# Four graph layers on one core: in the last layer VectorE masks messages by edge type, and sources are turned one chunk ahead

## The reference

```python
src = x[edge_src]
parts = [relu(x)]
for t in range(3):
    msg = relu(src @ W_e[t].T + b_e[t])
    msg = where((edge_type == t)[:, None], msg, 0)
    parts.append(segment_sum(msg, edge_dst))
agg = concatenate(parts, axis=1)
for t in range(3):
    o = agg @ W_n[t].T + b_n[t]
    updated = where((node_type == t)[:, None], o, updated)
x = layernorm(x + updated + x)
```

## Time and profile before

| | us |
|---|---|
| median of three runs | 2155.61 |
| the profiled execution | 2157.94 |
| its span | 2155.8 |
| busy in the span: TensorE, VectorE, ScalarE, GpSimd | 1613.2, 1479.8, 1087.1, 1385.2 |
| last layer: first product of its messages to the end of the span | 1714.1 to 2155.8 |

### The profile page before, as it was taken

How to read it: one execution, slowest core, us unless ns; L and a number is a source line. 1 busy time by engine, 2 the same in 40 slices (tenths; PEclk the granted TensorE clock), 3 DMA queues, 4 the chain that set the end, 5 groups by cost and what they waited for, 6 DMA issues and landing times.

```text
span 2155.8 us, 23908 instructions
## 1 busy us (share of the span) xinstructions
PE 1613.2 (75%) x6303; PEld 993.3 (46%) x6303; DVE 1479.8 (69%) x4219; ACT 1087.1 (50%) x2688; POOL 1385.2 (64%) x1060
## 2 busy tenths in 40 slices
PE   3777777777776377776776677777778499999995
PEld 1444444444444255555554344444444145555553
DVE  4788999988889377677776667776677444444453
ACT  0466666666666466777667243444343323233322
POOL 6888877788884667776660656555664146656663
PEclk7688888888888687888778788888889699999998
DMA  4333333333331344444443333333232122222221
GB/s 122 83 84 91 92 90 92 94 91 90 95 91 53 94 120 142 148 141 141 140 139 98 100 93 89 99 99 95 86 94 73 53 58 72 63 60 64 71 60 27
DMA packets 150726, 198.86 MB, mean 92 GB/s; under 512 B 54874, under 2 KB 82844, under 8 KB 150592
## 3 DMA queue, kind: packets, MB, share of 16 engines
q1 hardware_dynamic: 92992, 173.20, 25.7%
q0 software_dynamic: 57600, 24.15, 6.6%
HBM read 140.85 MB, written 70.88 MB: 98 GB/s over the span
## 4 chain that ended last, share of the span: by engine, by line
PE 58%; ACT 17%; issue 12%; DVE 7%; POOL 3%; DMA 2%; SPq 1%; POOLq 0%; ACTq 0%; DVEq 0%
PE po L1148 19%; PE pb L1342 10%; PE pt L1133 7%; ACT x L918 6%; PE po L1143 4%; ACT res L918 3%; PE pc L1133 3%; ACT st L973 3%; PE po L1207 2%; PE pb L1154 2%; DVE masked L838 2%; ACT do L918 1%; PE pc L1238 1%; ACT so L918 1%; PE pb L1379 1%
## 5 line engine op out<-in xcount | busy, mean ns | idle before, releaser
L434 POOL DMA_INDIRECT xs<-target_rows,slot_all x300 | 405.7, 1352 | 246.7 <-DMA xs<-source_rows 97.1
L918 ACT ACTIVATE x<-y,nmr,rst 125x128 f32<-125x128 f32 x800 | 318.5, 481 | 80.1 <-DVE nmr L671 80.0
L1148 PE MATMUL po<-wnt,rt 128*125 128x384 f32 x800 | 310.9, 537 | 0.2 <-ACT rt L948 0.2
L1133 PE MATMUL pt<-ident,x 125*128 125x125 f32 x800 | 144.2, 310 | 199.0 <-issue 182.4
L449 POOL TENSOR_TENSOR y<-xin,bias_bc 125x512 f32<-125x512 f32 x100 | 133.7, 1338 | 205.9 <-DMA xin<-in_x 201.4
L1148 PEld LDWEIGHTS po<-wnt,rt 128*125 128x125 f32 x800 | 174.2, 218 | 117.8 <-issue 40.8
L1342 PE MATMUL pb<-masked,wr 128*128 128x500 f32 x400 | 218.1, 709 | 1.5 <-DVE masked L838 1.5
L441 POOL DMA_INDIRECT out_rows<-do,last_all x100 | 120.2, 1202 | 145.2 <-ACT do L918 107.9
L838 DVE SCALAR_TENSOR_TENSOR masked<-rel,st 128x500 f32<-128x500 int32 x200 | 121.6, 670 | 132.8 <-ACT st L973 132.8
L1133 PEld LDWEIGHTS pt<-ident,x 125*128 125x128 f32 x800 | 105.2, 162 | 232.5 <-issue 207.0
L1143 PE MATMUL po<-ball,ones_bf 128*125 128x512 bf16 (+1 forms) x512 | 163.4, 452 | 51.1 <-DVE sel L688 48.7
(11 more groups left out here) (182 smaller groups left out, 3211.0 us busy)
## 6 DMA issues: line engine op xcount, KB each, us to landing
xin<-in_x SPq DMA_DIRECT2D x100, 250.0 KB
out_rows<-res SPq DMA_DIRECT2D x100, 250.0 KB
source_rows<-so SPq DMA_DIRECT2D x75, 250.0 KB
target_rows<-do SPq DMA_DIRECT2D x75, 250.0 KB
xs<-source_rows SPq DMA_DIRECT2D x75, 250.0 KB
xd<-target_rows SPq DMA_DIRECT2D x75, 250.0 KB
same<-same_d SPq DMA_DIRECT2D x75, 250.0 KB
aux<-start_d SPq DMA_DIRECT2D x25, 250.0 KB
```

What stands on the lines that cost most here:

```text
L434: return nc.gpsimd.indirect_dma_start(out=to, out_offset=None, in_=table, in_offset=bass.IndirectOffsetOnAxis(ap=index, axis=0), bounds_ch ...
L918: last = A(to[:, j, :], y[:, j, :], ACT.Identity, scale=rst[s][:, k:k + 1], bias=nmr[s][:, k:k + 1])
L1133: last = nc.tensor.transpose(tile_of(to, j), rows_[:, j, :], ident[0:R, 0:R])
L1148: last = mm(po[0:R, j * 512:j * 512 + NT * D], left(j), wnt[:, k, :, :].rearrange("k t d -> k (t d)"), start=False, stop=stop, skip_group_ ...
```

## The change

The offsets go: neither their table, its stores, its loads, nor the one-row products are there any more. The edge types are loaded for each chunk into all 128 partitions (`rel`, 250 KB) behind `same`, on the same semaphore, and VectorE multiplies each message by "type equals t" in place, all three types ahead of the three scans. TensorE turns the sources of chunk `c + 2` between the second and the third of the sums of chunk `c`, and ScalarE copies them at the end of its loop turn, ahead of `results3`. `sources3` no longer waits for the messages' products.

```diff
-            for t in range(NT):
-                sp.dma_start(off_d[t].rearrange("(p t) -> p t", t=PM), off_p[:, t, :]).then_inc(s_scr, 16)
-            sp.wait_ge(s_scr, 16 * (2 + NT))
+            sp.wait_ge(s_scr, 32)
...
             def sources3(c):
                 sp.wait_ge(q["tS"], at(c - 1))
-                sp.wait_ge(q["pM"], at((c - 1) * NT))
                 sp.dma_start(flat(xs[b]), rows(s_rows[2])[c]).then_inc(q["ld"][b], 16)
-                sp.dma_start(off[b][:, :, :], off_d[:, cols(c)][None]).then_inc(q["ld"][b], 16)
             def targets3(c):
                 sp.wait_ge(q["rd"], at(c - 1))
+                sp.wait_ge(q["vM"], at((c - 1) * NT))
                 sp.dma_start(flat(xd[b]), rows(d_rows[2])[c]).then_inc(q["aux"][b], 16)
                 sp.dma_start(same[b][:, :], to_all(same_d, c)).then_inc(q["aux"][b], 16)
+                sp.dma_start(rel[b][:, :], to_all(etype3, c)).then_inc(q["aux"][b], 16)
...
             def message_sums(c):
-                dve.wait_ge(q["aux"][b], counted(c, 32))
+                dve.wait_ge(q["aux"][b], counted(c, 48))
                 dve.wait_ge(q["pR"], at(c - 1))
                 for t in range(NT):
                     dve.wait_ge(q["eX"], c * NT + (t + 1))
+                    V.scalar_tensor_tensor(out=masked[:, t, :], in0=rel[b][:, :], scalar=float(t), in1=masked[:, t, :],
+                                           op0=ALU.is_equal, op1=ALU.mult).then_inc(q["vM"], 1)
+                for t in range(NT):
+                    dve.wait_ge(q["vM"], c * NT + (t + 1))
                     scan(m, t, same[b][:, :], masked[:, t, :], ALU.mult, ALU.add,
...
             for c in range(EC + 1):
                 if there(c + 1):
                     messages3(c + 1)
...
                 if there(c + 1):
                     targets3(c + 1)
+                if there(c + 2):
+                    evacuate_sources(c + 2, 3, 0)
                 if c >= 1:
                     results3(c - 1)
...
+            def turn_sources3(c):
+                pe.wait_ge(q["g"][b], counted(c, 16 * T))
+                pe.wait_ge(q["eD"], c)
+                turn(pt, xs[b]).then_inc(q["tS"], 1)
             def messages(c):
                 pe.wait_ge(q["eS"], c + 1)
                 for t in range(NT):
                     pe.wait_ge(q["eX"], at((c - 1) * NT + t + 1))
-                    mm(bank[5 + t][:, 0:C], ones_bf[0:1, :], off[b][0:1, t, :], start=True, stop=False)
-                    mm(bank[5 + t][:, 0:C], wet[:, t, :], st[:, :], start=False, stop=True).then_inc(q["pM"], 1)
+                    mm(bank[5 + t][:, 0:C], wet[:, t, :], st[:, :], start=True, stop=True).then_inc(q["pM"], 1)
             def targets(c):
-                pe.wait_ge(q["aux"][b], counted(c, 32))
+                pe.wait_ge(q["aux"][b], counted(c, 48))
                 pe.wait_ge(q["eS"], c + 1)
                 turn(pt, xd[b]).then_inc(q["tD"], 1)
...
                 for k in range(NT):
+                    if k == NT - 1 and there(c + 2):
+                        turn_sources3(c + 2)
                     pe.wait_ge(q["vA"], c * NT + (k + 1))
                     last = types(lambda j: run_tile(sums, k, j), 1 + k, stop=k == NT - 1)
```

More of the change, by code:

```diff
@@ L68, in gnn_kernel @@
     rdeg_d = nc.dram_tensor("rdeg_d", [1, E], F32).ap()
-    off_d = nc.dram_tensor("off_d", [NT, E], BF16).ap()
     slot_d = nc.dram_tensor("slot_d", [N, 1], I32).ap()
@@ L106, in gnn_kernel @@
         src_all, dst_all, nxt_all, last_all = (sb(n, [R, EC, T], I32) for n in ("src_all", "dst_all", "nxt_all", "last_all"))
-        ty = sb("ty", [R, PM], I32)
         same_p, start_p = (sb(n, [R, PM]) for n in ("same_p", "start_p"))
@@ L111, in gnn_kernel @@
         before_p, carry = sb("before_p", [R, 1]), sb("carry", [1, R + 1])
-        off_p = sb("off_p", [R, NT, PM], BF16)
         fill = sb("fill", [R, N // R], I32)
@@ L135, in gnn_kernel @@
         rel = two(sb, "rel", [D, C], I32)
-        off = two(sb, "off", [1, NT, C], BF16)
         run, run2 = sb("run", [D, 3, C + 1]), sb("run2", [D, 3, C + 1])
@@ L165, in gnn_kernel @@
         SINGLE = ("tS tD eS eD eL pA pB pR vA vE vL eX nS nD nF yb eN", "tS tD eS eD pR vA nS nD rd",
-                  "tS eS pM pR vA vM nD", "tS tD eS eD pM pR vA eX vN nD rd")
+                  "tS eS pM pR vA vM nD", "tS tD eS eD pM pR vM vA eX vN nD rd")
         PAIRS = ("aux g stS stD sc", "ld aux g stS stD", "ld aux rl g gi stD", "ld aux g sc")
@@ L204, in _ @@
             sp.dma_start(prv[0:1, 1:PM], bass.AP(dst.tensor, 0, [[PM, 1], [1, PM - 1]])).then_inc(s_idx, 16)
-            sp.dma_start(ty[:, :], pm(etype3)).then_inc(s_idx, 16)
             loads = [(ident[:, :], ident_d), (bias_bc[:, :], bias0[0:1, :].broadcast_to([R, D])),
@@ L470, in _ @@
             pool.wait_ge(s_const, 2)
-            pool.wait_ge(s_idx, 96)
+            pool.wait_ge(s_idx, 80)
             for j in range(T):
@@ L531, in updated @@
                 b, q = c % 2, ph[p]
-                pool.wait_ge(q["ld"][b], counted(c, 16 if p == 2 else 32))
+                pool.wait_ge(q["ld"][b], counted(c, 16))
                 for j in range(T):
@@ L581, in _ @@
             dve.wait_ge(s_const, 2)
-            dve.wait_ge(s_idx, 96)
+            dve.wait_ge(s_idx, 80)
             V.tensor_tensor(same_p[:, :], cur[:, :], prv[:, :], ALU.is_equal)
-            for t in range(NT):
-                V.tensor_scalar(off_p[:, t, :], ty[:, :], t, -BIG, ALU.not_equal, ALU.mult)
             V.tensor_copy(place[:, :], row_id[:, :])
@@ L1096, in messages3 @@
                 q = ph[3]
-                evacuate_sources(c, 3, 0)
                 for t in range(NT):
@@ L1111, in results3 @@
                 normalize(do[b], yd[b], b, 0).then_inc(q["nD"], 1)
+            evacuate_sources(0, 3, 0)
             messages3(0)
             targets3(0)
+            evacuate_sources(1, 3, 0)
             for c in range(EC + 1):
@@ L1367, in _, with messages @@
                 dense_products(d - 2)
-            def messages(c):
+            def turn_sources3(c):
                 b, q = c % 2, ph[3]
                 pe.wait_ge(q["g"][b], counted(c, 16 * T))
-                pe.wait_ge(q["ld"][b], counted(c, 32))
                 pe.wait_ge(q["eD"], c)
                 turn(pt, xs[b]).then_inc(q["tS"], 1)
+            def messages(c):
+                q = ph[3]
                 pe.wait_ge(q["eS"], c + 1)
@@ L1388, in _ @@
             pe.wait_ge(s_read, NC + 2 * LAG)
+            turn_sources3(0)
             messages(0)
             targets(0)
+            turn_sources3(1)
             for c in range(EC):
@@ L1420 @@
         "nextP": by_tile(np.append(a["dst"][1:], a["dst"].dtype.type(-1))), "eattrT": a["edge_attr_64"].T,
-        "etype3": a["edge_type_3"], "etype8": a["edge_type_8"][None], "eweight": a["edge_weight"][None],
+        "etype3": a["edge_type_3"][None], "etype8": a["edge_type_8"][None], "eweight": a["edge_weight"][None],
         "ntype3": a["node_type_3"][:, None], "ntypeP": by_row(a["node_type_3"]), "Wq": a["L0_gnn_Wq"], "Wk": a["L0_gnn_Wk"], "Wv": a["L0_gnn_Wv"],
```

## The result

The changed kernel takes 2199.86 us (median of 4 runs, 2198.37 to 2201.43); the kernel before, run beside it, 2155.69 (2153.47 to 2159.74). The ratio is 1.0203, with an interval of [1.0185, 1.0221]. The forecast was 2205. The profiled execution took 2201.43 us, its span is 2199.3.

The account below looks back on a forecast made before the run. Bound by TensorE's own work and, at nearly the same length, results read, targets loaded, turned, sums. 51 + 1.7 - 2 - 1.7 = +49 us on 2157.94 gives 2207, as median 2205 us; range 2168 to 2250.

Parts of the forecast that it names:

- Ring 1: Last layer: results read, targets loaded, targets turned, sums, with the sources' turn inside: 17.8 us a period.
- the price of the third transfer: Load of the targets: 256000 more bytes at 209 GB/s take 1.2 us more, so 5.4 + 1.2 = 6.6 us.
- the estimate from the Trainium skill: Load of `rel`: 8 rows of 2000 bytes on each engine, 0.55 us at 27 GiB/s; the load would be 6.0 us.
- The work of TensorE: TensorE in the last layer: its work of a period falls by 1.6 to 2.2 us.
- The price for the products: Three one-row products on TensorE: 0.93 us a period, or up to 0.6 more if the passes close up.
- The clock: TensorE's sums after idling: no loss to 3.4 us a period, taken as 1.1 us in the mean, about half losing.
- The wait of 2.8 to 3.4 us: TensorE stands idle this long each period, waiting for the load ahead of the turn of the targets.
- Ring 2: Sources' turn, copy, finished rows, scatters, gathers, next turn: 17.9 us, the least a period takes, with no load price in it.
- The masks: VectorE: three of 0.67 us, 2.0 us a period, hidden by the copy that stands ahead of the finished rows.
- The starts: Layer's start gains about 2 us, program's start 1.7 us, each with a range of 0 to 6.
- The sum of 49 us: Whole kernel: 51 + 1.7 - 2 - 1.7 = +49 us over the profiled execution's 2157.94 us.

Follow-up runs that it names:

- the added products: Kernel after, with three unused products of one tile put ahead of the turn of the targets: 2181.31 us, ratio 1.0136.
- the two kernels with third buffers: Third buffer for what the targets load, loads one chunk earlier: kernel before 2153.44 us; kernel after, sources' turn back at the messages, 2119.73 us.
- third buffers: Kernel after, with a third buffer for target rows and the tables loaded with them, loads issued one chunk earlier: 2188.25 us, ratio 1.0159.
- early types: Kernel after, with the load of the edge types moved to the earlier place of the source rows: 2198.99 us, ratio 1.0209.
- turn alone: Kernel before, offset table and one-row products kept, only the turn of the next sources and its copy moved as in the change: 2200.22 us, ratio 1.0207.
- the timed comparison: Kernel before, with only the three stores of the offset table moved from the program's start behind the first two feature loads: 2156.86 us, ratio 1.0008.
- the masks and two loads: Kernel after, with the types' load issued with the source rows and the sources' turn and copy back at the messages: 2141.08 us, ratio 0.9946.

## Why the prediction was right, and where it was not

*Ring 1.* Right in place and size: predicted 2.18 + 6.6 + 8.43 + 0.6 = 17.8 us, measured 17.74 in a period without loss of clock and 17.77 in the mean with the added products; the eight periods at a clock of 1.00 take 17.9 in the mean. The load took 6.62 (1927.56 to 1934.18) and 6.75 us, so the price of the third transfer from the rate in full flow, 1.2 us, was good. By the estimate from the Trainium skill, page "DMA: Bandwidth & Descriptors", section "Why a DMA increments its semaphore by 16 and not by 1", the load would have been 6.0 us; the measurement does not bear that out here.

*The work of TensorE.* Predicted to fall by 1.6 to 2.2 us; 1.31 in the profile after, 1.33 between the two kernels with third buffers. The price for the products (0.93, up to 0.6 more) was right, at 1.33. The rest was the wait for the copy, 0.68 us, which was idle time already and no work of TensorE's.

*The clock.* The wait of 2.8 to 3.4 us was 3.3. The loss, predicted as 1.1 us a period by a guess between nothing and 3.4, was 19.13 - 17.74 = 1.4, or 1.2 against the mean of 17.9. Here 15 periods of 23 lose clock, where the prediction had about half. That it is the clock, and goes when the idle time goes, is shown by the added products.

*Ring 2.* The step "no load price enters this ring, so 17.9 us is the least that a period takes" failed. 17.9 us is not the least: some periods take 17.6 us. The prediction put the whole copy between the turn and the finished rows, 0.95 + 0.59 = 1.54 us; where the turn waits for the gathers it is 1.16 (1939.86 to 1941.02), as ScalarE's rows start 0.48 us behind the start of the copy (1940.54). And the 7.73 us from gathers to turn, taken from the layer's start, where no scan runs beside the gathers, are not fixed: 7.97 in the kernel after (1931.89 to 1939.86), 8.56 with third buffers, 8.95 with early types (1947.07 to 1956.02). That makes it 18.3 us or more where this ring binds alone. The load has a part in it as far as it sets the time of VectorE's scans, beside which gathers take longer (last section). The prediction also left out what follows from 17.8 beside 17.9: neither ring alone is the cause. Three expectations, too (types early, third buffers, turn alone), were too low, since they took the second ring at 18.0 us or less. The change made two rings of 17.7 us, the load's by the third transfer and the turn within the sums, the scatters' by the turn's place and ScalarE's order. Opening one leaves the other, and only with both open is the saved work seen.

*The masks* cost nothing, as predicted: the finished rows start right behind the copy and not behind the scales.

*The starts.* Predicted 2 us for the layer's start and 1.7 for the program's. From the layer's first gather to the first read the profiles show 36.84 us before and 36.24 after, 0.6. The stores at the program's start are worth less than about 2 us by the timed comparison. The other 13.7 us of the profiled start are mostly the scatter between executions. The sum of 49 us against 43.5 (profiled) came out close with help from this: the periods cost 5 us more than predicted, the start gave 11 more.

## What to carry to other kernels

Before you take work from a busy engine, follow every ring that closes over a period through loads, scatters and gathers, and add each up: here the engine was 96% busy, a ring that is an estimated 0.3 us shorter (16.33 with the masks and two loads against 16.62) lay beneath it, the change made that longer and closed a second one. When two rings have one length, an experiment that opens one shows nothing; open both before calling either innocent. Load one chunk earlier before shortening what runs beside the load: that buffer alone was worth nothing before the change (ratio 0.9995), the change without it cost 2%, the masks with it gained 1.4 to 1.6%.

## What the runs showed of the hardware

Useless work raised the speed. The sums that took 7.46 us behind 3.24 us of idle time, at the granted clock 0.51, take 5.16 at 1.00; with the idle time partly filled by products that nobody uses, the clock stood at 1.00 throughout, and the kernel was 14 to 18 us faster. The length of one wait does not tell which period loses clock: behind 3.25 us (at 2101.87) turn and sums of that period ran at 1.00, behind 3.24 us (at 1913.78) they did not.

An indirect gather occupies GpSimd for a time that differs by kernel, with the same rows gathered: 1395 ns in the mean after the change, 1629 with early types, 1555 with third buffers. The loads beside the gathers don't explain it. With the finished rows first (ScalarE's order alone changed) the gathers are the shortest, 1305 ns in the mean, and there loads are issued close ahead of them, here 0.71 us (1919.65 to 1920.36), and the one that the masks wait for lands only at 1925.52:

```profile
1919.65 0.33 SPq L386 DMA_DIRECT2D xs<-source_rows  x1
...
1920.36 1.29 POOL L427 DMA_INDIRECT xs<-target_rows,slot_all  x1 [0.30 <-issue]
...
1921.96 1.29 POOL L427 DMA_INDIRECT xs<-target_rows,slot_all  x1 [0.30 <-issue]
1923.55 1.27 POOL L427 DMA_INDIRECT xs<-target_rows,slot_all  x1 [0.30 <-issue]
1925.13 1.28 POOL L427 DMA_INDIRECT xs<-target_rows,slot_all  x1 [0.30 <-issue]
1925.52 1.86 DVE L870 SCALAR_TENSOR_TENSOR masked<-rel,masked 128x500 f32<-128x500 int32 x3 [5.21 <-DMA rel<-in_etype]
```

What the long ones have beside them is VectorE's scans, here with early types (the three scans run from 1948.18 to 1951.74):

```profile
1947.07 1.29 POOL L427 DMA_INDIRECT xs<-target_rows,slot_all  x1 [0.30 <-issue]
1948.18 3.56 DVE L708 TENSOR_TENSOR_SCAN run<-same,run,masked 128x500 f32<-128x500 f32 x3 [1.88 <-DMA same<-same_d]
...
1948.67 1.86 POOL L427 DMA_INDIRECT xs<-target_rows,slot_all  x1 [0.30 <-issue]
...
1950.83 1.98 POOL L427 DMA_INDIRECT xs<-target_rows,slot_all  x1 [0.30 <-issue]
...
1953.12 1.27 POOL L427 DMA_INDIRECT xs<-target_rows,slot_all  x1 [0.30 <-issue]
```

In the fourteen profiles, 1800 to 2080, 231 of the 233 gathers with neither a scan nor a SCALAR_TENSOR_TENSOR of VectorE beside them take at most 1.30 us; of 397 that have scans beside them for over 0.5 us, 325 take over 1.35. No run moved the scans alone, so the cause is argued and not shown. Scatters did not change (1202, 1215, 1211 ns).
